# A two-layer graph network with a state-space scan on one core: x_proj as two column groups, other row ends, a later chunk 0, x on a second queue, an end in four buffers

## The reference

```
h = relu(adj @ x @ gcn_w + gcn_b);  h = layernorm(h) * ln_g + ln_b
xz = h @ w_in; xc, z = halves of 256
u = silu(causal conv of 4 taps over xc)
dbc = u @ w_xp                       # 8 columns for dt, 16 for B, 16 for C
dt = softplus(dbc[:, :8] @ w_dt + b_dt)
for every t and each of 16 states:  hst = exp(dt*A)*hst + dt*B*u;  y += hst*C
x1 = layernorm(x + (y + u*D_skip) * silu(z) @ w_out)
out1 = 3-layer relu MLP of scale1 * (adj @ x1);  out2 = the same with W2 of scale2 * (adj @ x2)
result = layernorm(x1 + concat(out1, out2) @ Wm.T + bm)
```

## Time and profile before

| | |
|---|---|
| median of 3 runs | 839.99 us (838.56 to 841.11) |
| the profiled execution | 837.98 us, its span 835.8 us |
| busy in the span | PE 811.0, POOL 661.3, DVE 597.7, ACT 375.0 us |
| adjacency blocks read | 144 MB, of 226.55 MB moved |

### The profile page before, as it was taken

How to read it: one execution, slowest core, us unless ns; L and a number is a source line. 1 busy time by engine, 2 the same in 40 slices (tenths; PEclk the granted TensorE clock), 3 DMA queues, 4 the chain that set the end, 5 groups by cost and what they waited for, 6 DMA issues and landing times.

```text
span 835.8 us, 7308 instructions
## 1 busy us (share of the span) xinstructions
PE 811.0 (97%) x2074; PEld 369.9 (44%) x2074; DVE 597.7 (72%) x798; ACT 375.0 (45%) x605; POOL 661.3 (79%) x322
## 2 busy tenths in 40 slices
PE   6999899999999999999999999999999999999995
PEld 2444334444444444434444444444444444444453
DVE  0020998789879878987888788888988898852135
ACT  0043574256534753565356535653466372301234
POOL 2001999999999999999999999989989999900046
PEclk9999999999999999999999999999999999999998
DMA  8987767766676688868776778699999999977602
GB/s 315 406 310 271 253 213 254 255 220 235 222 242 218 217 286 295 259 231 278 242 262 224 261 261 265 221 353 358 344 344 365 358 343 379 410 254 272 246 25 76
DMA packets 62956, 226.55 MB, mean 271 GB/s; under 512 B 7346, under 2 KB 8004, under 8 KB 44484
## 3 DMA queue, kind: packets, MB, share of 16 engines
q1 hardware_dynamic: 25668, 158.43, 51.4%
q10 hardware_dynamic: 37248, 67.65, 25.6%
HBM read 223.43 MB, written 2.62 MB: 270 GB/s over the span
## 4 chain that ended last, share of the span: by engine, by line
PE 86%; DVE 5%; ACT 3%; DMA 2%; issue 1%; POOL 1%; SPq 0%; ACTq 0%; POOLq 0%; DVEq 0%
PE p_x L469 45%; PE p_x L490 18%; PE p_two L490 8%; PE p_m L560 2%; DVE p_h L884 2%; PE p_m L576 2%; PE p_m L543 1%; PE p_dA L646 1%; DVE prod L893 1%; DVE p_two L902 1%; DMA ring<-adj_blocks 1%; PE p_two L550 1%; PE p_m L580 1%; PE p_m L526 1%; PE p_m L572 1%
## 5 line engine op out<-in xcount | busy, mean ns | idle before, releaser
L469 PE MATMUL p_x<-ring,x_s 128*128 128x512 f32 x1024 | 457.8, 597 | 9.9 <-DMA ring<-adj_blocks 8.1
L1057 POOL TENSOR_TENSOR y<-y,prod 128x1024 f32<-128x1024 f32 x127 | 299.8, 2361 | 18.5 <-DVE prod L893 18.5
L469 PEld LDWEIGHTS p_x<-ring,x_s 128*128 128x128 f32 x1024 | 194.8, 192 | 257.7 <-issue 250.4
L1048 POOL TENSOR_TENSOR bh<-spread,dtu 128x1024 f32<-128x1024 f32 x128 | 302.4, 2363 | 3.7 <-DMA spread<-bc_rows 3.7
L884 DVE TENSOR_TENSOR_SCAN p_h<-p_dA,state,bh 128x512 f32<-128x512 f32 x224 | 276.2, 1279 | 39.2 <-ACT p_dA L656 26.2
L656 ACT ACTIVATE p_dA<-dt,A 128x512 f32<-128x512 f32 x256 | 171.8, 687 | 152.8 <-DVE p_h L884 146.9
L490 PE MATMUL p_x<-ring,x 128*128 128x512 f32 x352 | 156.5, 593 | 1.7 <-issue 0.8
L893 DVE TENSOR_TENSOR prod<-p_h,spread_C 128x1024 f32<-128x1024 f32 x128 | 155.3, 1214 | 0.2 <-issue 0.2
L490 PEld LDWEIGHTS p_x<-ring,x 128*128 128x128 f32 x352 | 66.1, 190 | 84.2 <-issue 84.2
L401 POOL TENSOR_SCALAR mb<-prod,mv,rstd 128x128 f32<-128x128 f32 x28 | 21.8, 792 | 78.1 <-ACT rstd L871 77.5
L490 PE MATMUL p_two<-ring,x 128*128 128x512 f32 x160 | 72.6, 592 | 0.0
(11 more groups left out here) (119 smaller groups left out, 556.3 us busy)
## 6 DMA issues: line engine op xcount, KB each, us to landing
ring<-adj_blocks SPq DMA_DIRECT2D x143, 1024.0 KB, 7.0
spread<-bc_rows ACTq DMA_DIRECT2D x128, 256.0 KB, 4.7
spread_C<-bc_rows ACTq DMA_DIRECT2D x128, 256.0 KB, 5.6
x_s<-x_tiles SPq DMA_DIRECT2D x15, 256.0 KB, 8.6
out_tiles<-mb SPq DMA_DIRECT2D x8, 256.0 KB, 2.0
pack<-pack_w SPq DMA_DIRECT2D x1, 1026.5 KB, 13.6
ring<-adj_blocks SPq DMA_DIRECT2D x4, 256.0 KB, 3.6
bc_rows<-dbc ACTq DMA_DIRECT2D x8, 64.0 KB, 2.8
```

The costliest lines, as they stand in the source:

```text
L469: last = pe.matmul(bank[:, :], tiles[:, j, :], ring[:, i % RING, jt, :], start=j == 0, stop=j == N // P - 1)
L1048: pool.tensor_tensor(bh[:, i % 3, :, :], both(spread[:, i % SLOTS, :]), dtu[:, c % 2, :, :], ALU.mult).then_inc(s_bmul, 1)
L1057: pool.tensor_tensor(y[:, c % 2, :, :], y[:, c % 2, :, :], prod[:, i % 2, :, :], ALU.add).then_inc(s_acc, 1)
```

## The change

Five things change together.

1. x_proj. The weights wx3 have 64 columns instead of 128, with the dt columns once. Group 0's matmul writes rows 0 to 63 of p_m and group 1's rows 64 to 127, without accumulation. ScalarE copies 48 rows of the upper half to sq (step x_part); VectorE adds the lower half, those rows and the row of ones into dbc (x_sum); ScalarE sends B and C to DRAM and copies the nine dt rows to rows 64 to 72 (rows). On PE dt comes a half later, softplus, y_init, dt_sum and dtu one unit (dt_sum half a unit) later; x_proj counts 1 instead of 2 in `COST`. The filling around chunk 0's own x_proj is 5 and 3 tiles instead of 3 and 5.
2. Row ends. The last two blocks of a row of kind "one" are taken together: x of both, then x2 of both. In chunks 3 and 4 the second group of "two" blocks comes one block later.
3. In chunk 0 PE's gcn, cen, var, in_x, x_proj and dt go from halves 5, 7, 8, 10, 15, 16 to 6, 8, 10, 12, 16, 18.
4. x's 11 transfers and the packed weights are issued by ScalarE, before its first table load.
5. The end. `last_r`, mv and rstd have four buffers instead of two; the last tile is done in two halves, the first normalised by GpSimd, the second by VectorE, and sent in two transfers.

```diff
+XP = 64
+XP_ROWS = 16 + 2 * S
-FILL = {"gcn": 3, "cen": 3, "var": 5, "in_x": 13, "x_proj": 3, "dt": 5}
+FILL = {"gcn": 3, "cen": 3, "var": 5, "in_x": 13, "x_proj": 5, "dt": 3}
-        return ones[:1] + p + ones[1:6] + q + ones[6:]
+        return ones[:1] + p + ones[1:7] + q + ones[7:]
+        at = (6, 8, 10, 12, 16, 18) if c == 0 else tuple(2 * origin(c) + q for q in (-1, 1, 2, 4, 9, 11))
+        for name, q in zip(("gcn", "cen", "var", "in_x", "x_proj", "dt"), at):
+            put(q // 2, q % 2, name, c + 1)
-COST = {"z": 2, "out": 2, "in_x": 2, "x_proj": 2}
+COST = {"z": 2, "out": 2, "in_x": 2}
+        if kind == "one" and k == NBLK - 2:
+            parts += [(b, q) for lo in (0, JT) for b in (i, i + 1) for q in range(lo, lo + JT)]
+        elif kind != "one" or k < NBLK - 2:
+            parts += [(i, q) for q in range(len(block_steps(LOADS[i])))]
...
-            return prod[:, k % 2, 0, :].rearrange("p (t n) -> p t n", t=JT)
+            return prod[:, k % 4 // 2, k % 2, :].rearrange("p (t n) -> p t n", t=JT)
+        def end_parts(k):
+            if not 0 <= k < NC:
+                return []
+            if k < NC - 1:
+                return [(k, slice(0, JT))]
+            return [(k, slice(0, JT // 2)), (k + 1, slice(JT // 2, JT))]
...
-                        last = pe.matmul(p_m[:, :], wx3[:, g, :], u[:, g, :], start=g == 0, stop=g == G - 1)
+                        last = pe.matmul(p_m[XP * g:XP * (g + 1), :], wx3[:, g, :], u[:, g, :], start=True, stop=True)
...
-                    act.activation(dbc[:, :], p_m[:, :], ACT.Identity, bias=one_row[:, :]).then_inc(s_dbc, 1)
+                    act.activation(sq[0:XP_ROWS, :], p_m[XP:XP + XP_ROWS, :], ACT.Copy).then_inc(s_xpart, 1)
+                elif name == "rows":
+                    act.wait_ge(s_xsum, n + 1)
                     act.dma_start(rows_d[b], dbc[ROW_B:ROW_B + 2 * S, :]).then_inc(s_rows, 16)
+                    act.activation(dbc[ROW_DT[1]:ROW_DT[1] + R + 1, :], dbc[0:R + 1, :], ACT.Copy).then_inc(s_dbc, 1)
...
-                    put(o + 4, "x_proj", c + 1)
-                    put(o + 5, "softplus", c + 1)
-                    put(o + 6, "y_init", c + 1)
+                    put(o + 4, "x_part", c + 1)
+                    put(o + 5, "rows", c + 1)
+                    put(o + 6, "softplus", c + 1)
+                    put(o + 7, "y_init", c + 1)
...
+            for jt in range(JT):
+                act.dma_start(x_s[:, jt, :], x_d[0, :, jt]).then_inc(s_tile[jt], 16)
+            for k in range(1, NBLK):
+                act.dma_start(x_s[:, JT * k:JT * (k + 1), :], x_d[k]).then_inc(s_xs[k], 16)
+            act.dma_start(pack[:, :], pack_d).then_inc(s_pack, 16)
...
+                elif name == "x_sum":
+                    dve.wait_ge(s_xpart, n + 1)
...
+                    dve.scalar_tensor_tensor(out=dbc[0:XP_ROWS, :], in0=p_m[0:XP_ROWS, :], scalar=one_row[0:XP_ROWS, :],
+                                             in1=sq[0:XP_ROWS, :], op0=ALU.add, op1=ALU.add).then_inc(s_xsum, 1)
...
-                put(o + 6, 1, "dt_sum", c + 1)
+                put(o + 5, 0, "x_sum", c + 1)
+                put(o + 7, 0, "dt_sum", c + 1)
...
-                    wait(dve, s_fin, k - 1)
+                    wait(dve, s_fin, k - 3)
...
-            normalise(dve, NC - 1)
+            normalise(dve, NC - 1, range(JT // 2, JT), NC, s_fin_last)
...
-                    if c + 1 < NC and unit == origin(c) + 7:
+                    if c + 1 < NC and unit == origin(c) + 8:
...
+            normalise(pool, NC - 1, range(JT // 2), NC - 1, s_fin)
```

More of the change, by code:

```diff
@@ L352, in two_layer_graph_kernel @@
         s_z, s_zcopy, s_gate = sem("s_z"), sem("s_zcopy"), sem("s_gate")
[L353 removed]
+        s_dbcp, s_xpart, s_xsum, s_dbc = (sem(n) for n in ("s_dbcp", "s_xpart", "s_xsum", "s_dbc"))
         s_dtp, s_abs, s_sp, s_dt, s_dtu, s_yinit = (sem(n) for n in (
@@ L393, in fcount, with normalise, merge_bank @@
             return 0
-        def normalise(eng, k):
+        def normalise(eng, k, tiles, part, s_done):
             if k >= 2:
                 eng.wait_ge(s_out[k % 2], 16 * (k // 2))
[L399 to L403, removed]
+            eng.wait_ge(s_fv, 2 * part + 2)
+            for q in tiles:
+                last = eng.tensor_scalar(mb4(k % 2)[:, q, :], last_r(k)[:, q, :], mv[:, k % 4, q, 0:1],
+                                         rstd[:, k % 4, q:q + 1], ALU.subtract, ALU.mult)
+            last.then_inc(s_done, 1)
+        def end_parts(k):
[4 more added lines that the diff above has]
+            return [(k, slice(0, JT // 2)), (k + 1, slice(JT // 2, JT))]
         def layer_bank(l):
             return (p_dA[0][:, :], p_dA[1][:, :], p_h[:, 0, :])[l]
-        def merge_bank(k):
-            return (p_h[:, 1, :], p_m[:, :])[k % 2].rearrange("p (t n) -> p t n", t=JT)
+        def merge_bank(part):
+            return (p_h[:, 1, :], p_m[:, :])[part % 2].rearrange("p (t n) -> p t n", t=JT)
         block = ctx.enter_context(nc.Block())
@@ L630, in _ @@
                     pe.wait_ge(s_f, fcount(k, 2))
[L631 to L635, removed]
+                    for part, tiles in end_parts(k):
+                        wait(pe, s_fr, part - 1)
+                        for jt in range(JT)[tiles]:
+                            last = pe.matmul(merge_bank(part)[:, jt, :], sq[:, P * jt:P * (jt + 1)], Wm[:, 0, :],
+                                             start=True, stop=True)
+                        last.then_inc(s_mg, 1)
                 for l, src in ((2, ax[:, 1, :]), (1, hr[:, :]), (0, None)):
@@ L819, in _ @@
             take_x(0)
-            for name in ("gcn", "cen", "var", "in_x", "silu", "log_exp", "x_proj", "softplus", "y_init"):
+            for name in ("gcn", "cen", "var", "in_x", "silu", "log_exp", "x_part", "rows", "softplus", "y_init"):
                 step(name, 0)
@@ L865, in _ @@
                 k = t - 4
[L866 to L871, removed]
+                for part, tiles in end_parts(k):
+                    b = k % 4
+                    act.wait_ge(s_fst, 2 * part + 2)
+                    act.activation(rstd[:, b, tiles], mv[:, b, tiles, 1], ACT.Ln, bias=eps_t[:, :]).then_inc(s_fv, 1)
+                    act.wait_ge(s_fv, 2 * part + 1)
+                    act.activation(rstd[:, b, tiles], rstd[:, b, tiles], ACT.Exp, scale=-0.5).then_inc(s_fv, 1)
         @block.vector
@@ L990, in _ @@
             dve.wait_ge(s_two_add, 1)
-            for name in ("var", "taps0", "taps1", "dt_sum"):
+            for name in ("var", "taps0", "taps1", "x_sum", "dt_sum"):
                 step(name, 0)
@@ L1087, in _ @@
                                base=0, pattern=[[-1, P]], channel_multiplier=1).then_inc(s_cen_w, 1)
-            for q, row in enumerate(ROW_DT):
-                wait(pool, s_one_row, q)
-                pool.affine_select(out=one_row[:, :], in_=one_row[:, :], compare_op=ALU.not_equal, fill=1.0,
-                                   base=-(row + R), pattern=[[0, 1]], channel_multiplier=1).then_inc(s_one_row, 1)
+            pool.affine_select(out=one_row[:, :], in_=one_row[:, :], compare_op=ALU.not_equal, fill=1.0,
+                               base=-R, pattern=[[0, 1]], channel_multiplier=1).then_inc(s_one_row, 1)
             pool.memset(mean_w[:, :], 1.0 / D).then_inc(s_mean_w, 1)
@@ L1094, in _ @@
             pool.wait_ge(s_pack, 16)
-            for row in ROW_DT:
-                pool.tensor_copy(wx3[:, :, row:row + R], w_xp[:, :, 0:R])
+            pool.tensor_copy(wx3[:, :, 0:R], w_xp[:, :, 0:R])
             pool.tensor_copy(wx3[:, :, ROW_B:ROW_B + S], w_xp[:, :, R:R + S])
@@ L1117, in _ @@
             for k in range(NC - 1):
-                normalise(pool, k)
+                normalise(pool, k, range(JT), k, s_fin)
+            normalise(pool, NC - 1, range(JT // 2), NC - 1, s_fin)
 def kernel(**inputs):
```

65 lines of the change are left out of this document (32 added, 33 removed).

## The result

The changed kernel has a median of 834.71 us in 5 runs (832.23 to 836.52), beside 839.99 us (837.75 to 841.11) for the kernel before on the same chip: a ratio of 0.9952 (95% interval 0.9931 to 0.9972). The forecast was 833.8 us, range 829.5 to 838.0. It is not the only one: the shortest of copy_first's six runs, 829.51 us, has its lowest clock, 0.991. So the traces are read for what each part does, and the timed runs for the total.

What follows compares the result with a forecast made beforehand. PE's own work was taken as the bound until the last microseconds. Terms 1.0 + 1.1 + 3.4 + 0.5 - 1.9 + 3.2 - 1.1 = 6.2 us off 837.98 gave 831.8, plus 2.0 for the median: 833.8 us, range 829.5 to 838.0.

Steps and rivals of the forecast that it cites:

- x_proj: PE's x_proj in chunks 1 to 6: overlapping column groups cost 1.16 instead of 1.72 us, gaining 3.4 us.
- rival 1: At x_proj, column groups don't overlap or switching eats the saving: 4.0 us back, 837.8 us; chance 0.12.
- The further 0.5 us for dt's wait: PE ahead of dt: the 0.09 us dt waits today goes, six times, gaining 0.5 us.
- Row ends: PE's row ends: four waits for ScalarE's copy of p_x go, with slower passes, gaining 3.2 us.
- dt stalls: PE ahead of dt: waits of 1.1 to 1.2 us in chunk 6 and 0.7 in another chunk, together -1.9 us.
- the fourth row of the table: Stretch from in_x of chunk 6 to the last z: forecast 0.55 us longer than before.
- one other chunk: A chunk where PE has got ahead of the scans: a wait before dt, taken as 0.7 us.
- Chunk 0 later: Later PE steps in chunk 0 shrink the wait for hr; the lead kept at chunk 1 is 1.1 us.
- The stall at in_x of chunk 1: PE at in_x of chunk 1: waits for VectorE's hr, cutting earlier gains to 1.25 less about 0.1 us.
- Start: Start-up: x and weights on ScalarE's queue let SyncE issue blocks earlier, gaining 1.0 us.
- Rival 2: At the start, x and weights hold back the first blocks: -4.2 instead of +1.0, 839.0 us; chance 0.10.
- End: Final normalisation: GpSimd gets one half tile more and finishes last, costing 1.1 us.

Runs made afterwards that it cites:

- copy_first: Changed kernel with ScalarE's copy of the nine dt rows put ahead of the issue of the B and C rows: 830.15 us, 0.9906 of the kernel before.
- x_proj_alone: Kernel before with only the column groups, ScalarE's copies and VectorE's sum: 838.48 us, 0.9998 of the kernel before.
- x_proj_copy_first: Kernel before with column groups, copies and sum, the nine-row copy ahead of the B and C issue: 835.06 us, 0.9964 of the kernel before.
- dt_c0: Changed kernel with the nine-row copy ahead of the B and C issue and chunk 0's dt at 19, not 18: 830.56 us, 0.991 of the kernel before.
- old_end: Changed kernel with the end of the kernel before (two buffers, last chunk in one part): 831.34 us, 0.9922 of the kernel before.
- x_on_sync: Changed kernel with x and the weights issued on SyncE again: 837.47 us, 0.9981 of the kernel before.
- x_queue_alone: Kernel before with only x and the weights issued on ScalarE's queue: 836.26 us, 0.9979 of the kernel before.
- after_again: Changed kernel run again unaltered: 833.36 us, 0.9929 of the kernel before.
- dt_later: copy_first with dt one half later in chunks 0 (18 to 19) and 6 (19 to 20): 829.01 us, 0.9887 of the kernel before.
- row_ends_alone: Kernel before with only the new row ends (x, x, x2, x2): 834.25 us, 0.9947 of the kernel before.
- dt_c0_four_out: dt_c0 with four buffers for the normalised output tiles and output row 6 normalised on VectorE: 827.98 us, 0.988 of the kernel before.

## Why the forecast held

**The total** is right, and in part by luck. The sum gave 831.8 us for a profiled execution, and 2.0 were added because the runs of before had their median that much above its trace. The profiled execution of after took 836.52, 4.7 us more than the sum; but it is the longest of its five, with the median 1.8 below it, so the median missed by only 0.9. The sum by its terms does not stand in either trace of the changed kernel (1.1 and 2.1 us of span for 6.2). It nearly does in copy_first (7.5), which differs by one line's place, with a start that is 1.4 us better than forecast in it. No trace of one of the changed kernel's shorter runs was kept, so how much of the two stalls the median holds is not shown. (The chances for faster add to 0.58 + 0.15 + 0.11 = 0.84, not 0.83.)

**x_proj.** The column groups overlap, 1.01 us to the next instruction, so rival 1 falls. With 0.09 before them and 0.10 behind them the four passes cost 1.20 for 1.72: a gain of 0.52, where 0.56 was forecast. The further 0.5 us for dt's wait did not come. The forecast read the 0.09 ahead of dt as a wait for dbc; in after dbc is ready 0.8 us before dt, and the 0.09 is still there: it comes with going into row groups, as 0.09 comes with going into column groups, and is no wait. The chunks 2 to 5 accordingly give 0.50 each in x_proj_alone, not 0.65. That the five chunks gave 3.16 of 3.25 is luck: 0.64 of it is chunk 1's wait for ax, which belongs to the row ends.

**Row ends.** Right in kind and somewhat low: 3.6 instead of 3.2 when alone. With x_proj the five chunks give 6.1, where 3.16 and 3.59 apart would be 6.75; the 0.6 that is missing is chunk 1, which gives 1.15 with x_proj alone and 1.15 with both, as its one wait for ax can go only once.

**dt stalls.** This is the step that failed. The forecast had 627.85 as the time the copy is ready and 626.75 as the time dt is due, a stall of 1.1 to 1.2 us in chunk 6: scans, sum, then at once the copy. That chain is right only when the copy is issued at once: 1.12 us in x_proj_copy_first, 1.22 in copy_first. In the changed kernel the issue of the B and C rows, 0.91 us on ScalarE's queue, stands between, behind 0.45 us of an issue for the scans (621.77 to 622.22); both were in the program and neither was counted. Then PE waits 2.3 to 2.6 us, and the clock goes to its lower level for some microseconds, which the sum had nowhere: 3.4 to 3.6 us longer to the last z instead of 0.55. The forecast's term was -1.9; in after, the fourth row of the table alone is 2.8 worse than forecast, and the 0.7 for "one other chunk" was a wait of 2.93 us in chunk 0.

**Chunk 0 later.** The lead was taken as 1.1 us and chunk 0's dt was not looked at. Between gcn of chunk 0 and in_x of chunk 1 the lead is there when dt is one half later and waits no longer: 0.80 us in dt_c0, and 1.35, 1.07 and 1.52 in the three other kernels with that place. The stall at in_x of chunk 1 that the forecast asked for is there too, 0.97 us in copy_first and in dt_c0, and missing in after, where PE is behind VectorE (191.96 against 189.18 + 0.69). In the changed kernel the stall of 2.7 to 2.9 us and the passes at half speed behind it turn the lead into a loss of 0.8 to 1.0. Change 3 was never run alone. x_proj_copy_first has chunk 0's old places for all steps but dt, shows no stall of that kind at in_x, and has 0.82 us all the same; so what the later places bring by themselves is open.

**Start.** Right in sign, 1.5 us by the traces' means for 1.0. The Trainium skill, page "DMA: Bandwidth & Descriptors", Issuing engines are not separate DMA queues, has a second issuing engine save issue time alone; no run here separates that from bytes that come earlier, and in the stretch 14 to 18 us the transfers run at 418 GB/s in before and after alike, which agrees with it. Rival 2 falls. Block 1 near 12.4 us was asked for; in after it came at 13.21, in the other eight with x on ScalarE between 11.98 and 13.54.

**End.** Right: +1.0 and +1.3 in the two traces of the changed kernel, 0.9 between the means, for 1.1, with GpSimd as the last to work because mb has two buffers and its share grew.

## What to carry to other kernels

The issue of a transfer is an instruction of the engine that issues it: 0.33 to 1.36 us on ScalarE in the timelines read here. Put what the bound engine waits for ahead of it. A stall of TensorE costs more than its length when the clock falls behind it: with one of 2.44 us the stretch became 5.2 us longer in x_proj_alone. When a part of a change shows no gain, look in its trace for the one stretch that gives all back, before dropping the part. And when the last engine is found, count its operations, not only its buffers.

## What the runs showed of the hardware

Waits of much the same length were followed by both levels of the clock: 2.11 us at dt of chunk 0 in copy_first (1.00 behind it) and 2.20 us at dt of chunk 6 in old_end (0.61 in the window of 624 to 628 us); 2.16 us at 13 us in before (0.57) and 2.15 at the same place in x_on_sync (1.00); 2.81 us at dt of chunk 0 in x_on_sync (0.64 from 124 to 128 us) and 2.81 ahead of cen in chunk 0 in x_queue_alone (1.00 from 94 to 102). So the loss is not a fixed price of a wait. It may be a part of the scatter between runs (5.3 us between the shortest and the longest of after_again, 2.9 in dt_later, 1.3 in row_ends_alone), but not all of it: dt_c0_four_out, whose waits of PE from 40 to 780 us are all under 1.6 us, scatters by 4.7 us at clocks of 0.995 to 0.999. The same transfer of the B and C rows took 0.48 us to issue in chunk 4 of after, 0.91 in chunk 6, and 1.36 in chunk 6 of x_proj_copy_first.
